# Cross-attention and routed experts: the table of expert slots kept in SBUF

## The reference, cut to what matters

```python
x = x + xattn(layernorm(x), ctx, Wq, bq, Wk, bk, Wv, bv, Wo, bo)
# experts, on y = layernorm(x), n_tokens = 8192, E = 8, capacity 1024
weights = router(y, embeddings)              # softmax over the two best of 8
ones = (weights > 0)
cap_ones = where(cumsum(ones, axis=0) <= expert_capacity, ones, 0.0)
vals, idx = top_k((weights * cap_ones).T, expert_capacity)
tokens = y[idx]                              # [8, 1024, 512]
inter = relu(einsum('ech,eih->eci', tokens, first_linear))
out = einsum('eci,ehi->ech', inter, second_linear) * vals[:, :, None]
x = x + zeros.at[idx].add(out)
```

## Time and profile before

| what | value |
|---|---|
| median of three runs | 1715.33 us (1706.84 to 1718.24) |
| the profiled execution | 1708.75 us, its span 1707.0 us |
| first stage, to the last `sidx` | 0 to 982.7 us of the span |
| from there to the first product of expert 0 | 982.7 to 1028.4 us |
| experts | 1028.4 to 1707.0 us |
| busy in the span | PE 85%, DVE 66%, POOL 51%, ACT 49% |

### The profile page before, as it was taken

The page is one execution under the profiler, slowest core; times in us unless marked ns, Lnnn a source line. Parts: engine busy times, 40 slices in busy tenths (PEclk is TensorE's granted clock), DMA queues, the critical chain, the costliest instruction groups (busy, mean ns, idle before and its releaser), DMA issues.

```text
span 1707.0 us, 23602 instructions
## 1 busy us (share of the span) xinstructions
PE 1448.7 (85%) x8551; PEld 869.3 (51%) x8551; DVE 1126.1 (66%) x2063; ACT 835.0 (49%) x1700; POOL 864.0 (51%) x807
## 2 busy tenths in 40 slices
PE   4466999988899888869786609999999999999996
PEld 2254767666666666656564303444444444444443
DVE  4685999998898987879887613544545454545431
ACT  1474787775676766667673223323333333334220
POOL 3263667666888568856685753141414232323211
PEclk8687999998899989989998858999999999999999
DMA  5125646636888447663546347556555556555411
GB/s 197 36 60 116 185 116 166 166 107 105 146 134 148 130 96 136 111 140 95 114 98 126 82 66 189 158 157 157 166 145 156 144 153 148 155 144 159 94 45 44
DMA packets 325839, 217.32 MB, mean 127 GB/s; under 512 B 266121, under 2 KB 266505, under 8 KB 325722
## 3 DMA queue, kind: packets, MB, share of 16 engines
q1 hardware_dynamic: 305091, 165.00, 43.1%
q0 software_dynamic: 19456, 50.73, 10.5%
q10 hardware_dynamic: 1175, 0.07, 0.0%
HBM read 105.65 MB, written 50.95 MB: 92 GB/s over the span
## 4 chain that ended last, share of the span: by engine, by line
PE 49%; DVE 20%; issue 10%; ACT 7%; DMA 6%; POOL 5%; SPq 2%; ACTq 0%; POOLq 0%; DVEq 0%
PE ps L1189 20%; PE ps L1207 19%; ACT sd L669 3%; DMA xt<-x 3%; PE ps L715 3%; PE ps L596 2%; DVE sd L640 2%; DVE mx L650 2%; DVE ph L697 2%; PE ps L736 2%; DVE sm L678 2%; DVE x L743 1%; POOL tab_dram L918 1%; DVE st6b L519 1%; DMA pT<-ph 1%
## 5 line engine op out<-in xcount | busy, mean ns | idle before, releaser
L1189 PE MATMUL ps<-xT,w1s 128*128 128x512 f16 x1536 | 335.1, 381 | 47.1 <-DMA xT<-xh 47.1
L1207 PE MATMUL ps<-w2s,hT 128*128 128x512 f16 x1536 | 332.8, 379 | 0.0
L1189 PEld LDWEIGHTS ps<-xT,w1s 128*128 128x128 f16 x1536 | 150.6, 98 | 230.0 <-issue 50.2
L1195 ACT ACTIVATE hT<-ps 128x512 f16<-128x512 f32 x128 | 76.4, 597 | 360.8 <-PE ps L1189 360.8
L1207 PEld LDWEIGHTS ps<-w2s,hT 128*128 128x128 f16 x1536 | 150.3, 98 | 181.2
L596 PE MATMUL ps<-xnT,wqh 128*128 128x256 f16 x1536 | 193.0, 280 | 33.5 <-DVE xnT L576 22.7
L715 PE MATMUL ps<-pT,vb 128*128 128x256 f16 (+1 forms) x1248 | 177.9, 298 | 42.9 <-issue 17.6
L1217 POOL DMA_INDIRECT out_dram<-ys,idx x64 | 71.3, 1114 | 277.8 <-DVE ys L1212 273.4
L669 ACT ACTIVATE sd<-sd,nb,lim 128x77 f32<-128x77 f32 x512 | 185.3, 444 | 49.2 <-DVE nb L654 49.0
L596 PEld LDWEIGHTS ps<-xnT,wqh 128*128 128x128 f16 x1536 | 151.0, 100 | 66.6 <-DVE xnT L576 29.4
L1197 DVE SCALAR_TENSOR_TENSOR hT<-ps,hT 128x512 f16<-128x512 f32 x128 | 87.7, 689 | 145.0 <-ACT hT L1195 145.0
(11 more groups left out here) (155 smaller groups left out, 2228.5 us busy)
## 6 DMA issues: line engine op xcount, KB each, us to landing
xs<-x SPq DMA_DIRECT2D x64, 256.0 KB, 2.9
xt<-x SPq DMA_DIRECT2D x64, 256.0 KB, 4.8
out_dram<-x SPq DMA_DIRECT2D x64, 256.0 KB, 5.3
xrow_dram<-x SPq DMA_DIRECT2D x64, 256.0 KB, 3.9
stage<-w1T SPq DMA_DIRECT2D x8, 2048.0 KB, 9.5
stage<-w2T SPq DMA_DIRECT2D x8, 2048.0 KB, 8.5
tab_dram<-ids,sidx POOLq DMA_INDIRECT x128
wqf<-wq SPq DMA_DIRECT2D x1, 1024.0 KB, 7.9
```

What stands on the lines that cost most here:

```text
L1189: do("pe", lambda q, k=k, a=a, b=b, i=i, last=last: q.matmul(hb[z][:, :], w1s[e % 2][:, a, k, ic * P:(ic + 1) * P], xT[:, 4 * b + k, cols] ...
L1207: do("pe", lambda q, k=k, a=a, b=b, i=i, last=last: q.matmul(yb[z][:, :], hT[:, a, k, s * P:(s + 1) * P], w2s[e % 2][:, b, k, :], start=(k ...
```

## The change

The table in DRAM, its 128 indirect writes, its first filling and the read back are gone. In their place the list is built in SBUF as `acc` (128 partitions x 64 columns: slot / 8 is the row, expert * 8 + slot % 8 the column). For each tile and choice POOL makes two one-hot matrices: `pick` (128 x 128, the row) and `put` (128 x 64, the column, times the token's number counted down from the end of its sequence). PE multiplies them, four products per pair of tiles summed in `bM` (`invert`, L942), and DVE adds the sum to `acc` (L946). Every slot is hit by one token at most, so the sum is the token's number; at the end of a sequence 2048 is added to what is filled (L951, L954). `rank2` ends with six DVE instructions (L907 to L920) in place of four. `rs1` and `nm1` now share the memory of `mv1`, and `onesf` that of `pick`. In the scheduler's tables `onehot` has rank 149.48 and cost 1.0 per tile, `invert` rank 149.6 and cost 0.1; `scatter` had rank 149.48 and cost 1.25 per DMA. No other rank changes.

```diff
-    "v_route": "lgc m8 ix n2w dd ef oh den gw vd mask gd cumr pm cum pk okf gq sx idx",
-    "v_stats": "lns lna l2s l2a nw nwr1",
+    "v_route": "lgc m8 ix n2w dd ef oh den gw vd mask gd cumr pm cum pk pi hc hcf row sx",
+    "v_stats": "lns lna l2s l2a nw nwr1 acc top up idx",
...
-        iota = sb("iota", [P, E], F32)
-        ids = sb("ids", [P, T], I32)
-        empt = sb("empt", [P, 64], I32)
+        iota = sb("iota", [P, P], F32)
+        local = sb("local", [P, TPB], F32)
+        loi = sb("loi", [P, TPB], I32)
...
+        acc = sb("acc", [P, 64], F32)
+        top = sb("top", [P, 64], F32)
...
-        rs1 = sb("rs1", [P, T], F32)
-        nm1 = sb("nm1", [P, T], F32)
+        rs1, nm1 = mv1[:, :, 1], mv1[:, :, 0]
...
+        rowf = sb("rowf", [P, 2, RMAXN, 2], F32)
+        colf = sb("colf", [P, 2, RMAXN, 2], F32)
+        pick = sb("pick", [P, 2, TG, 2, P], F16)
+        place[0] -= 2048
+        onesf = sb("onesf", [P, P], F32)
+        place[0] += 1536
+        put = sb("put", [P, 2, TG, 2, 64], F16)
...
+        do("pool", lambda e: e.iota(loi[:, :], [[-P, TPB]], base=SEQ, channel_multiplier=-1), mark=("c_i", 5))
+        do("pool", lambda e: e.tensor_copy(local[:, :], loi[:, :]), after=[("c_i", 5)], mark=("c_i", 6))
...
-            do("dve", lambda e: e.scalar_tensor_tensor(okf[:, 0:n, :], pk[:, 0:n, :], float(CAP), vd[:, 0:n, :],
-                                                       ALU.is_le, ALU.mult), after=[("pk", G)], mark=("okf", G))
-            yield
-            do("dve", lambda e: e.scalar_tensor_tensor(gq[:, 0:n, :], ef[:, 0:n, :], float(CAP), pk[:, 0:n, :],
-                                                       ALU.mult, ALU.add), after=[("pk", G)], mark=("gq", G, 0))
-            yield
-            do("dve", lambda e: e.scalar_tensor_tensor(gq[:, 0:n, :], gq[:, 0:n, :], -1.0 - EMPTY, okf[:, 0:n, :],
-                                                       ALU.add, ALU.mult), after=[("okf", G), ("gq", G, 0)],
-               mark=("gq", G, 1))
-            yield
-            do("dve", lambda e: e.tensor_scalar(sidx[:, t0:t1, :], gq[:, 0:n, :], float(EMPTY), None, ALU.add),
-               after=[("gq", G, 1)], mark=("sx", G))
-
-        def scatter(t, k):
-
-            dma("pool", lambda q: q.indirect_dma_start(
-                tab, bass.IndirectOffsetOnAxis(sidx[:, t, k:k + 1].bitcast(U32), 0), ids[:, t:t + 1], None,
-                bounds_check=E * CAP - 1, oob_is_err=False), ("sct", t, k), 0,
-                after=[("sx", span_of[t]), ("l_tab",), ("c_i", 5)])
-
+            was = ("put", r_span[G - 2][1] - 1, 1) if G > 1 else None
+            do("dve", lambda e: e.tensor_scalar(pi[:, 0:n, :], pk[:, 0:n, :], -1.0, None, ALU.add),
+               after=[("pk", G)], mark=("pi", G))
+            yield
+            do("dve", lambda e: e.tensor_scalar(hc[:, 0, 0:n, :], pi[:, 0:n, :], 3, None, ALU.arith_shift_right),
+               after=[("pi", G)], mark=("hc", G, 0))
+            do("dve", lambda e: e.tensor_scalar(hc[:, 1, 0:n, :], pi[:, 0:n, :], 7, None, ALU.bitwise_and),
+               after=[("pi", G)], mark=("hc", G, 1))
+            yield
+            do("dve", lambda e: e.tensor_copy(hcf[:, 0:n, :], hc[:, 1, 0:n, :]), after=[("hc", G, 1)],
+               mark=("hcf", G))
+            do("dve", lambda e: e.tensor_copy(rowf[:, G % 2, 0:n, :], hc[:, 0, 0:n, :]), after=[("hc", G, 0), was],
+               mark=("row", G))
+            yield
+            do("dve", lambda e: e.scalar_tensor_tensor(colf[:, G % 2, 0:n, :], ef[:, 0:n, :], 8.0, hcf[:, 0:n, :],
+                                                       ALU.mult, ALU.add), after=[("hcf", G)], mark=("sx", G))
+
+        def onehot(t):
+
+            G, j = divmod(t, TG)
+            R = span_of[t]
+            row, col = rowf[:, R % 2, t - r_span[R][0], :], colf[:, R % 2, t - r_span[R][0], :]
+            for k in range(2):
+                do("pool", lambda e, k=k: e.tensor_scalar(pick[:, G % 2, j, k, :], iota[:, :], row[:, k:k + 1],
+                                                          None, ALU.is_equal),
+                   after=[("sx", span_of[t]), back("inv", G, 2), ("esum",), ("c_i", 6)], mark=("pick", t, k))
+                do("pool", lambda e, k=k: e.tensor_scalar(put[:, G % 2, j, k, :], iota[:, 0:64], col[:, k:k + 1],
+                                                          local[:, t % TPB:t % TPB + 1], ALU.is_equal, ALU.mult),
+                   mark=("put", t, k))
+
+        def invert(G):
+
+            b = G * TG // TPB
+            slots = bM[:, 256:320]
+            todo = [(j, k) for j in range(TG) for k in range(2)]
+            for i, (j, k) in enumerate(todo):
+                do("pe", lambda e, i=i, j=j, k=k: e.matmul(slots, pick[:, G % 2, j, k, :], put[:, G % 2, j, k, :],
+                                                           start=(i == 0), stop=(i == len(todo) - 1)),
+                   after=[("put", TG * G + j, k), free["M"]], mark=("inv", G) if i == len(todo) - 1 else None)
+            free["M"] = ("acc", G)
+            do("dve", lambda e: e.tensor_tensor(acc[:, :], slots, acc[:, :], ALU.add),
+               after=[("inv", G), ("s_z", 2), ("acc", G - 1) if G else None, ("up", b - 1) if b else None],
+               mark=("acc", G))
+            if (G + 1) * TG % TPB == 0 and b < B - 1:
+                yield
+                do("dve", lambda e: e.tensor_scalar(top[:, :], acc[:, :], 0.0, float(SEQ), ALU.is_gt, ALU.mult),
+                   after=[("acc", G)], mark=("top", b))
+                yield
+                do("dve", lambda e: e.tensor_tensor(acc[:, :], acc[:, :], top[:, :], ALU.add), after=[("top", b)],
+                   mark=("up", b))
...
-        stage("scatter", scatter, per(T, 2), at=[t + RG[span_of[t]] for t in range(T) for _ in range(2)])
+        stage("onehot", onehot, per(T), at=[t + RG[span_of[t]] for t in range(T)])
+        stage("invert", invert, per(NG), at=[t + RG[span_of[t]] for t in range(TG - 1, T, TG)])
...
-        def load_idx(lo, hi):
-            dma("sp", lambda q: q.dma_start(idx[:, 8 * lo:8 * hi].rearrange("p (e s) -> p e s", s=8),
-                                            tab[CAP * lo:CAP * hi, :].rearrange("(e b s) c -> b e (s c)", b=P, s=8)),
-                ("l_idx", lo), lo, after=[("sct", T - 1, 1)])
-            do("dve", lambda e: e.tensor_scalar(gix[:, 8 * lo:8 * hi], idx[:, 8 * lo:8 * hi], float(N - 1), None, ALU.min),
-               after=[("l_idx", lo)], mark=("idx", lo))
-
-        load_idx(0, 1)
-        load_idx(1, E)
+        do("dve", lambda e: e.tensor_scalar(idx[:, :], acc[:, :], -1.0, float(N), ALU.mult, ALU.add),
+           after=[("acc", NG - 1)], mark=("idx", 0))
+        do("dve", lambda e: e.tensor_scalar(gix[:, :], idx[:, :], float(N - 1), None, ALU.min), after=[("idx", 0)],
+           mark=("idx", 1))
...
-                    after=ATT_DONE + [("idx", min(e, 1)), ("xlo", e - 1, s) if e else None,
+                    after=ATT_DONE + [("idx", 1), ("xlo", e - 1, s) if e else None,```

The order on POOL where the list of the first group begins, ahead of the change: `tab_dram` is the table, and each such row is one indirect DMA.

```order
L918 DMA tab_dram<-ids,sidx 8192x1
L617 TENSOR_TENSOR qT<-part,qT 128x256
L617 TENSOR_TENSOR oT<-part,oT 128x256
L918 DMA tab_dram<-ids,sidx 8192x1
L658 TENSOR_TENSOR sd<-sd,mx 128x616
L617 TENSOR_TENSOR qT<-part,qT 128x256
L918 DMA tab_dram<-ids,sidx 8192x1 x5
```

39 lines of the change are left out of this document (16 added, 23 removed).

## The result

The changed kernel takes 1720.84 us in the median of nine runs (1717.03 to 1728.61), the kernel before 1714.01 in as many (1706.84 to 1718.24). The ratio is 1.0054, with a 95% interval of 1.003 to 1.0078: no gain, but a small loss of half a per cent. The forecast was 1658 with a range of 1620 to 1697. The profiled execution of after takes 1718.26 us, its span 1716.5.

A forecast was written before the change was run, and what follows sets the result against it. The first stage was taken to run at DVE's pace until table writes slowed it, with x landing late. 1708.75 - 18 - 36 = 1654.75 us from the profiled execution, 1661 from the median; 1658 was taken, range 1620 to 1697.

The forecast's parts named there:

- the price of a one-hot: On POOL, 0.29 and 0.18 us for the two kinds, 0.94 us per tile, 60 us for 64 tiles.
- Term 2: First stage before the experts: 48 us of slowdown put on table writes, less 12 us of DVE work, gains 36 us.
- 22.5 us per pair: First stage before any table write: time per pair of tiles, taken as DVE's pace.
- Term 1: Where first stage meets experts: last group's chain to the first gather takes 3.7 us instead of 22.5; 18 us counted.
- The backlog of earlier groups is gone too: Behind POOL's last attention instruction: 28 one-hots (7 us) stand in place of 23 DMAs (29 us).
- PE stops at the inversions: PE's in-order queue: each of 32 inversions waits for POOL's last `put`, stalling attention products; slower, 1741 us, chance 6%.
- The excess goes entirely: First stage: all 78 us above its clean pace vanish, plus 18 where the stages meet; 1613 us, chance 12%.
- DVE is held by the one-hots: First stage: all 60 us of one-hot time stops DVE, cancelling the gains; 1715 us, no change, chance 7%.
- Only the joint gains: First-stage pace stays, from new order or added DVE time; only the stages' meeting point gains 18 us; 1691, chance 17%.
- the 13 that I read out of the earlier trace: L697 on DVE: one-hots bring back its slower time, 0.32 us for some 40 tiles, 13 us; kept for the range.
- 24 us per pair: Sign of being right: first stage from 390 to 930 us runs at about 24 us per pair of tiles.
- x still late: Sign of failing as a whole: loads of x land late without table writes, so the first-stage gain would vanish.

The follow-up runs named there:

- a_short: Changed kernel in its own order, products, additions and waits kept, each one-hot comparison replaced by a memset of the same tile, lists constant; 1658.0 us, ratio 0.9704.
- b_none: Kernel before in its own order, without the table's fill, indirect writes and read back, lists constant; 1637.67 us, ratio 0.9492.
- b_port: Kernel before in its own order, each table write replaced by two POOL memsets, no fill or read back, lists constant; 1683.56 us, ratio 0.9744.
- a_pe: Changed kernel without its one-hots, `pick` and `put` cleared once, products and additions kept, lists constant; 1658.25 us, ratio 0.9709.
- a_none: Changed kernel in its own order without one-hots, products and additions, lists constant; 1654.87 us, ratio 0.9591.
- a_pool: Changed kernel with one-hots kept on POOL, their products and additions left out, lists constant; 1703.81 us, ratio 0.9861.
- a_memset: Changed kernel without products and additions, lists constant, each POOL one-hot replaced by a 592-column memset that reads nothing; 1696.09 us, ratio 0.9903.
- a_dve: Changed kernel, nothing left out, all 256 one-hots on DVE instead of POOL, scheduler's cost 0.8 per tile; 1716.4 us, ratio 1.0016.

## Why the prediction was wrong, by its own steps

**What failed: the price of a one-hot.** "Its nearest rows are a select over 128 x 128 at 0.29 us and an iota over 128 x 64 at 0.18", and from them 0.94 us per tile and "64 x 0.94 = 60 us for 173". The comparison takes 0.603 and 0.588 us, so 2 x (0.603 + 0.588) = 2.4 us per tile and 152 us in all by the medians. By the means it is 167, which the 14 long ones raise. This one term was off by a factor of 2.5 to 2.8 (152 / 60 and 167 / 60). It was the term I had bounded least: "If a one-hot costs twice the rows, the joint still gains 16.9" asks the question for the joint and not for the body, where 64 tiles hang on it. a_short puts the price back, at 0.204 and 0.151 us, and comes to 0.9704 for the predicted 0.967. That it meets the number to the microsecond is luck: in the body the table writes cost more than foreseen (55 for 48), the order took 17 us where the prediction had nothing, and products and additions took, by the body, about nothing where it had 12. So 39.8 us came out for 36, while the joint gave 15.9 for 18. The memsets are also a little cheaper than the 0.29 and 0.18 us of the prediction. The step that failed is still this one price; put right alone, it turns the loss into the forecast gain.

**Term 2, what the excess is made of.** "48 us stay for the table writes" was nearly right as a size: b_none shows 55. But I gave it all to the DMAs, since x landed late. b_port shows two causes in it, 32 us from the DMAs (across groups) and 24 from POOL being taken; the rise of POOL's busy time from 15.5 to 20.6 us per pair stood in the same paragraph and got no share. The first cause went as foreseen. The second grew from 24 to 44 us with 168 us of one-hots in its place, the order added 17 and products and additions some 10: 32 - 20 - 17 - 10 = -15, for a body that was measured 15.6 us longer. These parts are all differences of the same six bodies, so that they add up is so by construction and no check on them; the ones across groups, 32 and 10, carry the doubt. The order the prediction had at zero, products and additions at 12; "its order changes from the first one-hot on" was named, without a price. What stands at the bottom of the body is also not the 22.5 us per pair from which the excess was counted: without any list work b_none needs 552.0 / 22.5 = 24.5.

**Term 1, the joint.** Between `colf` and the gather 6.7 us were measured for 3.7, nearly all of the difference from the price: eight one-hots take 1012.43 + 0.59 - 1008.43 = 4.6 us for 1.9. The rest is right. Missed was what is ahead of it, 6.5 us more between the last residual and the last `colf`, where the last group's routing on DVE stands behind an `acc` that waits for POOL. The price has 3.0 of them, since a_short still needs 14.0; 13.5 pass in a_pe without any one-hot and 12.2 in a_none without any list work, so about 1.7 are the order's (across groups). "The backlog of earlier groups is gone too" holds for the way to the gather, where POOL idled 5.71 us ahead of its last eight one-hots, and not for the routing ahead of `colf`.

**The rivals.** *PE stops at the inversions* (6%, 1741 us) names the place that comes into being: PE waits 31.4 us 23 times for `put` in the whole execution and DVE 45.7 us 15 times for the products that it adds to `acc`. It doesn't decide by itself: with the same waits in the order, a_short is at 1658, with 14.6 and 20.0 us of them. They grow with the price. *The excess goes entirely* (12%, 1613 us) did not come: no kernel here, not even b_none without any list work (0.9492, which is 1627 of 1714), is as fast. What it said of the clock did, at the short price: 0.99 and 0.98 in a_short. *DVE is held by the one-hots* (7%, 1715 us) came closest to the time and by another mechanism. L700, the old L697, does get longer, 1834 ns in the mean for 1662, but in a_none, without any one-hot, it is as long:

```profile
L729 DVE SCALAR_TENSOR_TENSOR ph<-sd,ph 128x1232 f16<-128x1232 f32 x64 | 118.3, 1849 | 8.9 <-ACT ph L725 8.7
```

So the split does take some 11 us more of DVE than before (172 ns times 64), close to the 13 that I read out of the earlier trace rows, but not because of the one-hots. In after 14 splits begin beside a one-hot and take 1.48 us in the mean; 11 begin beside the normalization L691 on POOL and take 2.9. By the Trainium skill, SBUF — State Buffer, section "Who interferes with whom", the split contends with a GpSimd instruction that reads SBUF, and one of the two waits. The trace agrees, and shows that with the one-hots it is POOL that waits: 13 of the 14 one-hots over 0.7 us lie beside a split. So the rule bore on this change by the other engine than the prediction feared: it lengthened the one-hots by some 14 us in all. *Only the joint gains* (17%, 1691 us) had the body unchanged, which is nearer to what happened than the forecast, though its reason, the order, is 17 of the 36 + 15.6 = 52 us by which the body missed.

**The signs that were named.** Of the list under "What would show it", the landing of x (3.2 us), ACT's waits and the experts (678.3 us) came out right; the one-hot at 0.2 to 0.3 us, the gather within 5 us and 24 us per pair came out wrong. Two signs of its list for being wrong are there: PE waits for `put`, and DVE waits to form `acc`. The sign named for failing as a whole, x still late, was the wrong one: x is early and term 2 vanished all the same.

## What to carry to other kernels

An operation that no row shows must be priced by one that does the same arithmetic, not by one of the same shape, and where it occurs hundreds of times its upper bound goes through the whole sum, not through one term. When a stretch slows down with two things at once (DMAs late and an engine fuller), divide the excess between both before one is removed, since the replacement may keep the other. And a new operation's cost in a scheduler's table wants measuring first: here the one number was worth 2% of the kernel, more than the change itself gained in the end. Last, parts that are differences of the same few measurements always add up; compare them within one group of runs before they are believed.

## What the runs showed of the hardware

- A comparison with `tensor_scalar` on POOL takes 0.527 to 0.603 us over 128 x 128 and 0.578 over 128 x 64, where a copy takes 0.291 and a memset 0.204; on DVE the same comparison takes 0.286.
- A one-hot on POOL that runs beside the split on DVE, which has two inputs in SBUF, is drawn out from 0.6 us to between 1.5 and 1.9 (13 times in after, 15 in a_pool), while the split beside it takes 1.43 to 1.64 in after; a memset of 0.592 us, which reads nothing, never takes over 0.66 (a_memset). With the one-hots on DVE 33 of 256 take over 0.7 us, each beside a computing instruction of POOL (a_dve).
- 128 indirect writes of 128 rows each slow the other DMAs: x lands after 6.9 us beside them and after 3.1 to 3.6 us where they are left out or replaced, the transposes after 6.9 and 5.1 (b_port). Some 32 us of the stage go with it, by bodies across groups, beside 24 for POOL being taken.
- POOL's time has no fixed price at this pace: 45.5 us more are free (a_short), 178 us cost 24 us in before's order (b_port), 168 us cost 44 in after's (a_pool), where they lie in runs of up to 20 ahead of the last residual.
